# Mixture-of-experts layer on one core: tiles of 128 tokens, two tiles of any two experts per step, in place of pairs of tiles of one expert

## The chip, the cores and the metric

One core of one Trainium2 chip runs the program. The metric is the device time of one execution in microseconds, the median of the runs shown.

## The reference

The input is 8 sequences of 512 tokens with 256 features, fp32. A block of linear attention comes first and is not touched here; its result is added to the input and normalized. Then every token goes to 4 of 16 experts and to one shared expert:

```
weights, indices = gate(x)            # top 2 of 4 groups, then top 4 of 16 experts
h1 = x @ w1[e]; h3 = x @ w3[e]        # 256 -> 128, for the 4 chosen e
y  = sum_e c[e] * ((silu(h1) * h3) @ w2[e])        # 128 -> 256
z  = (silu(x @ ws1) * (x @ ws3)) @ ws2             # shared expert, 256 -> 256 -> 256
out = layernorm(x + y + z)
```

## The kernel before

All five queues are written out by hand, with semaphores between them. The work has three stages.

**Head (0 to 266 us).** Eight batches of 512 tokens pass through attention, first norm and routing. VectorE gives every (token, expert) a slot in a DRAM buffer `expert_in` with one region per expert (`assign_slots`), and GpSimd scatters the token rows there with indirect DMAs (`dispatch`, line 440). The batches form two waves of four; each wave has its own buffers. When a wave's counts are known, `plan_pairs` (lines 816 to 860) computes on VectorE which expert and which DRAM row each step takes: the region of an expert is cut into pairs of 256 rows, and the pairs of all experts are numbered through. With 64 tiles' worth of tokens and one partly filled pair per expert that makes at most 32 + 16 = 48 pairs per wave, and the program always runs all 48. Rows that no token fills are zeroed by SyncE (`fill_spare`, `fill_end`). The plan of wave 0 stands between the last batch and the shared expert (line 976); that of wave 1 is spread over the steps of wave 0 (`parts`, line 1089).

**Pair loop (266 to 593 us).** 96 steps, one pair each. For step g:
- SyncE (`load_xs`, line 325) reads the row from `pair_row` into a register, waits until the ring slot's earlier pair is transposed, and loads 256 rows (256 KB) into one of four `xs` tiles (in `kv`). `store_ys` (line 332) stores the result of an older pair.
- TensorE (`two_groups`, line 1375) transposes pair g + 2 (line 1340), reads the chunk number, that is the expert, of pair g into a register (`chunk_of`, line 1345), multiplies up (`up_pair`, line 1347) and then multiplies down pair g - 2 (`down_pair`, line 1360). Weights are split in a high and a low 16-bit part, and so are activations, so each product is three matmuls (`product`, lines 1149 to 1151). `we_hi[:, chunk, cols]` is addressed through the register. The loop body holds 8 steps; its first two read the chunk of pair g - 2 again.
- ScalarE splits and copies (lines 617, 624, 634, 642), VectorE forms the low parts and the product with silu (lines 1025, 1036, 1044).
- In wave 1, VectorE also adds wave 0's gathered results (`combine`) and normalizes them (`final_norm`, line 1065); GpSimd gathers them with indirect DMAs (line 452), each tile when `h_ready` reaches a number written in the program.

**Tail (593 to 705 us).** The last batches' shared expert, wave 1's gathers, combines and norms.

SyncE, ScalarE, VectorE and TensorE all write the loop in the same order of steps, most of it in hardware loops (`Fori`).

## Time and profile before

| | |
|---|---|
| median of 3 runs | 711.87 us (711.7 to 711.9) |
| the profiled execution's own time | 707.36 us |
| its span, first to last instruction | 705.5 us |
| granted TensorE clock, mean | 0.916 |
| busy: PE, DVE, ACT, POOL | 527.1, 427.4, 300.1, 290.1 us |
| bytes moved | 118.63 MB, mean 168 GB/s |

```text
span 705.5 us, 13461 instructions
## 1 busy us (share of the span) xinstructions
PE 527.1 (75%) x3532; PEld 357.0 (51%) x3555; DVE 427.4 (61%) x1200; ACT 300.1 (43%) x659; POOL 290.1 (41%) x334
## 2 busy tenths in 40 slices
PE   1899887889897688789786688798888779665400
PEld 1355443555544357567574566576667566421300
DVE  2447783776864866666554444377757556652784
ACT  2536653436524343555454555356546445110100
POOL 1000126456446402454444200644446251777574
PEclk9999997899999899999999999899999989977755
DMA  7022428295451303767767766687787753333332
GB/s 202 13 75 76 156 90 284 82 304 209 177 185 68 103 18 106 239 204 230 232 228 259 238 223 216 180 235 233 211 261 231 223 181 134 105 120 89 94 114 99
DMA packets 64091, 118.63 MB, mean 168 GB/s; under 512 B 9760, under 2 KB 23088, under 8 KB 64048
## 3 DMA queue, kind: packets, MB, share of 16 engines
q1 hardware_dynamic: 51216, 84.55, 37.1%
q0 software_dynamic: 12288, 33.57, 15.1%
q8 instruction: 19, 0.31, 0.2%
q14 instruction: 24, 0.20, 0.1%
q10 hardware_dynamic: 544, 0.00, 0.0%
HBM read 55.17 MB, written 62.91 MB: 167 GB/s over the span
## 4 chain that ended last, share of the span: by engine, by line
PE 36%; DVE 19%; issue 15%; SPq 9%; another core or an unknown queue 6%; ACT 6%; DMA 5%; POOL 4%; ACTq 0%; DVEq 0%; POOLq 0%
PE t L1340 4%; PE h_even L1149 4%; PE h_even L1151 4%; PE h_odd L1149 3%; PE h_even L1150 3%; PE h_odd L1151 3%; PE h_odd L1150 3%; DVE x_all L1055 2%; SPq L327 2%; PE y L1186 2%; DMA kv<-expert_in 2%; SPq L330 1%; PE y L1373 1%; SPq L334 1%
## 5 line engine op out<-in xcount | busy, mean ns | idle before, releaser
L440 POOL DMA_INDIRECT expert_in<-x_all,slots x128 | 132.9, 1038 | 117.8 <-PE h_odd L1151 45.0
L452 POOL DMA_INDIRECT wa_stage<-expert_out,result_of x64 | 62.9, 983 | 35.3 <-issue 18.1
L1340 PE MATMUL t<-ident,kv 128*128 128x128 f32 x384 | 60.3, 280 | 19.4 <-DMA kv<-expert_in 15.0
L452 POOL DMA_INDIRECT q_fm<-expert_out,result_of x32 | 32.4, 1014 | 85.6 <-DMA expert_out<-q_exp 63.9
L426 POOL TENSOR_SCALAR neg_mean<-mv 128x4 f32<-128x4 f32 x16 | 4.6, 290 | 149.5 <-DVE mv L699 149.3
L1044 DVE TENSOR_TENSOR wa_lo<-bias_heads,wa_hi 128x256 bf16<-128x256 f32 x96 | 40.5, 422 | 41.3 <-ACT wa_hi L642 30.1
L1149 PE MATMUL h_even<-xsT_hi,we_hi 128*128 128x256 f16 x192 | 54.3, 283 | 10.7 <-issue 8.8
L1340 PEld LDWEIGHTS t<-ident,kv 128*128 128x128 f32 x384 | 45.3, 145 | 26.8 <-DMA kv<-expert_in 12.1
L1025 DVE TENSOR_TENSOR xsT_lo<-t,xsT_hi 128x512 bf16<-128x512 f32 x72 | 49.5, 688 | 11.6 <-ACT xsT_hi L617 5.9
L1150 PE MATMUL h_even<-xsT_lo,we_hi 128*128 128x256 bf16 x192 | 54.2, 282 | 2.5 <-issue 2.5
L1151 PE MATMUL h_even<-xsT_hi,we_lo 128*128 128x256 f16 x192 | 54.2, 282 | 1.4 <-issue 1.4
L617 ACT ACTIVATE xsT_hi<-t 128x512 f16<-128x512 f32 x72 | 42.0, 585 | 16.6 <-PE t L1340 12.8
L642 ACT ACTIVATE wa_hi<-bias_heads 128x256 f16<-128x256 f32 x96 | 39.7, 414 | 20.7 <-DVE bias_heads L1036 14.4
L1036 DVE TENSOR_TENSOR bias_heads<-h_odd,kv_heads 128x256 f32<-128x256 f32 x48 | 20.2, 420 | 41.8 <-ACT kv_heads L634 40.9
L1036 DVE TENSOR_TENSOR bias_heads<-h_even,kv_heads 128x256 f32<-128x256 f32 x48 | 20.1, 419 | 34.4 <-ACT kv_heads L634 30.9
L634 ACT ACTIVATE kv_heads<-h_odd 128x256 f32<-128x256 f32 x48 | 18.3, 381 | 52.8 <-remote 25.0
L1186 PE MATMUL y<-wo_sb,gated 128*128 128x256 f32 x128 | 33.3, 419 | 9.3 <-DVE gated L686 9.3
L452 POOL DMA_INDIRECT gate<-expert_out,result_of x32 | 30.5, 954 | 19.4 <-PE h_even L1151 10.0
L529 ACT ACTIVATE kv<-h_even 128x256 f32<-128x256 f32 x32 | 12.3, 386 | 58.3 <-PE h_even L1151 52.4
L634 ACT ACTIVATE kv_heads<-h_even 128x256 f32<-128x256 f32 x48 | 18.2, 380 | 43.8 <-PE h_even L1151 17.4
L1367 PE MATMUL y<-we_hi,wa_hi 128*128 x96 | 26.8, 279 | 12.6 <-issue 10.7
L624 ACT ACTIVATE k_exp<-y 128x512 f32<-128x512 f32 x48 | 28.7, 598 | 15.9 <-PE y L1373 14.3
(222 smaller groups left out, 1530.0 us busy)
## 6 DMA issues: line engine op xcount, KB each, us to landing
kv<-expert_in SPq DMA_DIRECT2D x96, 256.0 KB
expert_out<-k_exp SPq DMA_DIRECT2D x48, 256.0 KB
expert_out<-q_exp SPq DMA_DIRECT2D x48, 256.0 KB
expert_in<-wa_stage SPq DMA_DIRECT2D x16, 512.0 KB
expert_in<-wa_stage SPq DMA_DIRECT2D x32, 256.0 KB
stage<-in_L_ffn_w SPq DMA_DIRECT2D x48, 128.0 KB
x_in<-in_L_attn_x SPq DMA_DIRECT2D x8, 512.0 KB
out<-gated SPq DMA_DIRECT2D x8, 512.0 KB
```

The costliest lines, as they stand in the source:

```text
L440: pool.indirect_dma_start(xs_dram[b // WB], bass.IndirectOffsetOnAxis(ap=slots[:, b, t, j:j + 1], axis=0), x_all[:, b, t, :], None).then_i ...
L452: pool.indirect_dma_start(y_got[i][:, j, :], None, ys_dram[w], bass.IndirectOffsetOnAxis(ap=result_of[:, b, t, j:j + 1], axis=0)).then_inc ...
L617: act.activation(xsT_hi[r][:, :, :], t_bank[r % 2][:, :].rearrange("p (c n) -> p c n", c=KC), ACT.Copy).then_inc(xst_hi_ready, 1)
L642: act.activation(aT_hi[r % 2][:, :], a_pair, ACT.Copy).then_inc(at_hi_ready, 1)
L1025: dve.tensor_tensor(xsT_lo[r][:, :, :], t_bank[r % 2][:, :].rearrange("p (c n) -> p c n", c=KC), xsT_hi[r][:, :, :], ALU.subtract).then_in ...
L1036: dve.tensor_tensor(a_pair, h_banks[r % 2][0][:, 2 * P:], s_pair, ALU.mult).then_inc(pair_a_ready, 1)
L1044: dve.tensor_tensor(aT_lo[r % 2][:, :], a_pair, aT_hi[r % 2][:, :], ALU.subtract).then_inc(at_lo_ready, 1)
L1149: pe.matmul(dst, sta_hi, mov_hi, start=start, stop=False)
L1150: pe.matmul(dst, sta_hi, mov_lo, start=False, stop=False)
L1151: return pe.matmul(dst, sta_lo, mov_hi, start=False, stop=stop)
L1186: last = pe.matmul(y_bank[h][:, (t % 2) * D:(t % 2 + 1) * D], gated[:, c, t * P:(t + 1) * P], wo_sb[:, c, :], start=c == 0, stop=c == KC - 1)
L1340: last = pe.transpose(t_bank[r % 2][:, c * 2 * P + i * P:c * 2 * P + (i + 1) * P], xs[r][:, i, c * P:(c + 1) * P], ident[:, :])
```

## The change

A step takes two tiles of 128 rows, each of any expert. Tiles are numbered through all experts, at most 64 + 16 = 80 per wave, and step p of a wave takes tiles p and p + 40: 40 steps a wave, 80 in all. Each tile has its own chunk and its own row. SyncE reads two rows and loads two halves of the `xs` tile (64 partitions with two rows each); the transposes write to every second column so that the halves stay apart; TensorE reads two chunks and multiplies up and down once per tile, with 128 columns in place of 256 in the up product. The plan works on 80 tiles per wave instead of 48 pairs and has one step more; the results' rows get one more operation. Half as many spare rows are zeroed. The 16 fills of wave 1's ends begin two groups earlier. GpSimd's fixed numbers change with the step count, and it waits for `out_ready` before three of its norm computations. The norms of wave 0's first three batches move from VectorE to ScalarE, and ScalarE's and VectorE's second wave is written out in place of hardware loops; the combines are spread evenly, from step 4 of the wave on.

```diff
-PLAN_STEPS = 8
+PLAN_STEPS = 9
...
-    NPAIR = WT * TOP_K // 2 + E
+    NTILE = WT * TOP_K + E
+    NPAIR = NTILE // 2
     PAIR = 2 * P
-    MOST = WB * S // PAIR
-    REGION = (MOST + 1) * PAIR
-    SPARE = NPAIR - WT * TOP_K // 2
-    SLOTS = E * REGION + SPARE * PAIR
+    MOST = WT
+    REGION = (MOST + 1) * P
+    SPARE = NTILE - WT * TOP_K
+    SLOTS = E * REGION + SPARE * P
     RING = 4
     GROUPS_OF_PAIRS = NPAIR // RING
     EARLY = WB - 1
-    PLAN_GROUPS = 7
+    PLAN_GROUPS = 8
+    NORM_PAIR = 17
     FILL_ROWS = 512
-    FILLS = SPARE * PAIR // FILL_ROWS
+    FILLS = SPARE * P // FILL_ROWS
...
-        pair_chunk = sb("pair_chunk", [1, WAVES * NPAIR, 1], I32)
-        pair_row = sb("pair_row", [1, WAVES * NPAIR, 1], I32)
+        tile_chunk = sb("tile_chunk", [1, 2, WAVES * NPAIR, 1], I32)
+        tile_row = sb("tile_row", [1, 2, WAVES * NPAIR, 1], I32)
...
             def load_xs(w, p, r, first=False):
-                row = sp.value_load(pair_row[0:1, NPAIR * w + p, :], min_val=0, max_val=SLOTS - PAIR)
+                rows = [sp.value_load(tile_row[0:1, h, NPAIR * w + p, :], min_val=0, max_val=SLOTS - P) for h in range(2)]
                 if not first:
                     sp.wait_ge(xs_transposed, NPAIR * w + p - RING + 1)
-                sp.dma_start(xs[r][:, :, :], rows_of(xs_dram[w], row)).then_inc(xs_loaded[r], 16)
+                for h in range(2):
+                    sp.dma_start(xs[r][h * P // 2:(h + 1) * P // 2, :, :],
+                                 rows_of(xs_dram[w], rows[h])).then_inc(xs_loaded[r], 16)
...
-                    pool.wait_ge(h_ready, NPAIR + (3 * k if k < WT - TT else 3 * WT - 13 + 2 * (k - WT + TT)))
+                    pool.wait_ge(h_ready, NPAIR + 9 * k // 4)
...
-                    pool.wait_ge(h_ready, 5 * i // 2)
+                    pool.wait_ge(h_ready, 2 * i)
...
-                        if b > 0 and t == (1 if w == 0 else TT - 1):
+                        if b > 0 and t == (2 if w == 0 else TT - 1):
+                            if 1 < b <= EARLY + 1:
+                                pool.wait_ge(out_ready, b - 1)
...
+            def final_norm(b, t):
+                if t == 0:
+                    act.wait_ge(rstd_ready, NB + b + 1)
+                    if b > 0:
+                        act.wait_ge(out_stored, 16 * b)
+                last = act.activation(o_sb[:, t, :], x_all[:, b, t, :], ACT.Identity, bias=shift[:, t:t + 1],
+                                      scale=rstd[:, t:t + 1])
+                if t == TT - 1:
+                    last.then_inc(out_ready, 1)
...
-            with act.Fori(1, all_groups // 2 - 1) as q2:
+            with act.Fori(1, GROUPS_OF_PAIRS // 2) as q2:
                 group(2 * q2)
                 group(2 * q2 + 1)
-            group(all_groups - 2)
-            group(all_groups - 1, last=True)
+            for p in range(NPAIR):
+                pair(NPAIR + p, p % RING, GROUPS_OF_PAIRS + p // RING, p < NPAIR - 2)
+                b, t = (p - NORM_PAIR) // 9, (p - NORM_PAIR) % 9
+                if 0 <= b < EARLY and t < TT:
+                    final_norm(b, t)
...
                 if part == 5:
                     dve.wait_ge(plan_step, at + 6)
-                    dve.scalar_tensor_tensor(closer[:, w, :], first_pair[:, :], float(PAIR), region_start, ALU.mult, ALU.subtract)
-                    dve.tensor_reduce(pair_expert_f[:, :], ended, AX_X, ALU.add)
-                    dve.tensor_tensor(skipped, ended, region_left[0:1, :].unsqueeze(1).to_broadcast([1, NPAIR, E]),
-                                      ALU.mult).then_inc(plan_step, 1)
+                    dve.scalar_tensor_tensor(closer[:, w, :], first_tile[:, :], float(P), region_start, ALU.mult, ALU.subtract)
+                    dve.tensor_reduce(tile_expert_f, ended, AX_X, ALU.add).then_inc(plan_step, 1)
                 if part == 6:
                     dve.wait_ge(plan_step, at + 7)
-                    dve.tensor_reduce(pair_row_f[:, :], skipped, AX_X, ALU.add).then_inc(plan_step, 1)
-                    dve.tensor_scalar(pair_chunk[:, NPAIR * w:NPAIR * (w + 1), 0], pair_expert_f[:, :], float(E - 1), float(SHARED),
+                    dve.tensor_tensor(ended, ended, region_left[0:1, :].unsqueeze(1).to_broadcast([1, NTILE, E]),
+                                      ALU.mult).then_inc(plan_step, 1)
+                    dve.tensor_scalar(tile_chunk[:, :, NPAIR * w:NPAIR * (w + 1), 0],
+                                      tile_expert_f.rearrange("p (h g) -> p h g", h=2), float(E - 1), float(SHARED),
                                       ALU.min, ALU.add).then_inc(experts_ready, 1)
                 if part == 7:
                     dve.wait_ge(plan_step, at + 8)
-                    dve.scalar_tensor_tensor(pair_row[:, NPAIR * w:NPAIR * (w + 1), 0], pair_no[0:1, :], float(PAIR),
-                                             pair_row_f[:, :], ALU.mult, ALU.add).then_inc(rows_ready, 1)
+                    dve.tensor_reduce(tile_row_f, ended, AX_X, ALU.add).then_inc(plan_step, 1)
+                if part == 8:
+                    dve.wait_ge(plan_step, at + 9)
+                    dve.scalar_tensor_tensor(tile_row[:, :, NPAIR * w:NPAIR * (w + 1), 0],
+                                             tile_no[0:1, :].rearrange("p (h g) -> p h g", h=2), float(P),
+                                             tile_row_f.rearrange("p (h g) -> p h g", h=2), ALU.mult, ALU.add).then_inc(rows_ready, 1)
...
+            group(PLAN_GROUPS + 1)
             dve.wait_ge(c_of_slot_ready, NB // 2)
             dve.wait_ge(shared_added, EARLY)
-            thirds = [((), (0,), (1, 2), (3, 4)), ((5,), (6,), (7, 8), (9,)), ((10,), (11, 12), (13,), (14, 15))]
-            halves = [[(8 * h + 2 * r, 8 * h + 2 * r + 1) for r in range(RING)] for h in range(2)]
-            group(q1)
-            for i in range(3):
-                group(q1 + 1 + i, 0, thirds[i])
-            with dve.Fori(1, EARLY) as b:
-                group(q1 + 1 + 3 * b, b, thirds[0])
-                group(q1 + 2 + 3 * b, b, thirds[1], norm=b - 1)
-                group(q1 + 3 + 3 * b, b, thirds[2])
-            group(q1 + 1 + 3 * EARLY, EARLY, halves[0], whole=False)
-            group(q1 + 2 + 3 * EARLY, EARLY, halves[1], norm=EARLY - 1, whole=False, last=True)
+            of_pair = [[i for i in range(WT * TOP_K) if 4 + 9 * i // 16 == p] for p in range(NPAIR)]
+            for p in range(NPAIR):
+                add = [(i // 16, i // TOP_K % TT, i % TOP_K) for i in of_pair[p]]
+                pair(NPAIR + p, p % RING, p < NPAIR - 2, add)
...
             def transpose_xs(g, r, use):
-                pe.wait_ge(xs_loaded[r], 16 * use)
+                pe.wait_ge(xs_loaded[r], 32 * use)
                 for c in range(KC):
+                    turned = t_bank[r % 2][:, c * PAIR:(c + 1) * PAIR].rearrange("p (k t) -> p k t", t=2)
                     for i in range(2):
-                        last = pe.transpose(t_bank[r % 2][:, c * 2 * P + i * P:c * 2 * P + (i + 1) * P],
-                                            xs[r][:, i, c * P:(c + 1) * P], ident[:, :])
+                        last = pe.transpose(turned[:, :, i], xs[r][:, i, c * P:(c + 1) * P], ident[:, :])
                 last.then_inc(xs_transposed, 1)
-            def chunk_of(g):
-                return pe.value_load(pair_chunk[0:1, g, :], min_val=SHARED, max_val=NCH - 1)
-            def up_pair(g, r, chunk):
+            def chunks_of(g):
+                return [pe.value_load(tile_chunk[0:1, h, g, :], min_val=SHARED, max_val=NCH - 1) for h in range(2)]
+            def up_pair(g, r, chunks):
                 if late(g, 2):
                     pe.wait_ge(pair_a_ready, g - 1)
-                for k in range(2):
-                    for c in range(KC):
-                        cols = slice((c * 2 + k) * INTER, (c * 2 + k + 1) * INTER)
-                        last = product(h_banks[r % 2][0][:, k * PAIR:(k + 1) * PAIR],
-                                       we_hi[:, chunk, cols], we_lo[:, chunk, cols],
-                                       xsT_hi[r][:, c, :], xsT_lo[r][:, c, :], c == 0, c == KC - 1)
+                for h, chunk in enumerate(chunks):
+                    tok = slice(h * P, (h + 1) * P)
+                    for k in range(2):
+                        for c in range(KC):
+                            cols = slice((c * 2 + k) * INTER, (c * 2 + k + 1) * INTER)
+                            last = product(h_banks[r % 2][0][:, k * PAIR + h * P:k * PAIR + (h + 1) * P],
+                                           we_hi[:, chunk, cols], we_lo[:, chunk, cols],
+                                           xsT_hi[r][:, c, tok], xsT_lo[r][:, c, tok], c == 0, c == KC - 1)
                 last.then_inc(h_ready, 1)
-            def down_pair(g, r, chunk):
+            def down_pair(g, r, chunks):
                 pe.wait_ge(at_lo_ready, g + 1)
                 if late(g, 2):
                     pe.wait_ge(ys_copied, g - 1)
-                w2_hi, w2_lo = we_hi[:, chunk, W13:], we_lo[:, chunk, W13:]
-                dst, tok = y_bank[r % 2][:, 0:D], slice(0, P)
-                pe.matmul(dst, aT_hi[r % 2][:, tok], w2_hi, start=True, stop=False)
-                pe.matmul(dst, aT_lo[r % 2][:, tok], w2_hi, start=False, stop=False)
-                pe.matmul(dst, aT_hi[r % 2][:, tok], w2_lo, start=False, stop=True)
-                dst, tok = y_bank[r % 2][:, D:], slice(P, PAIR)
-                pe.matmul(dst, aT_hi[r % 2][:, tok], w2_lo, start=True, stop=False)
-                pe.matmul(dst, aT_hi[r % 2][:, tok], w2_hi, start=False, stop=False)
-                pe.matmul(dst, aT_lo[r % 2][:, tok], w2_hi, start=False, stop=True).then_inc(ys_ready, 1)
+                for h, chunk in enumerate(chunks):
+                    last = product(y_bank[r % 2][:, h * D:(h + 1) * D],
+                                   aT_hi[r % 2][:, h * P:(h + 1) * P], aT_lo[r % 2][:, h * P:(h + 1) * P],
+                                   we_hi[:, chunk, W13:], we_lo[:, chunk, W13:], True, True)
+                last.then_inc(ys_ready, 1)
             def two_groups(q, last=False):
                     pe.wait_ge(xst_lo_ready, g + 1)
                     if not (last and i >= 2 * RING - 2):
                         transpose_xs(g + 2, (r + 2) % RING, q + 1 + (i + 2) // RING)
-                    chunks.append(chunk_of(g))
+                    chunks.append(chunks_of(g))
                     up_pair(g, r, chunks[i])
                     if i >= 2:
                         down_pair(g - 2, (r - 2) % RING, chunks[i - 2])
                     elif late(q, 1):
-                        down_pair(g - 2, (r - 2) % RING, chunk_of(g - 2))
+                        down_pair(g - 2, (r - 2) % RING, chunks_of(g - 2))
                 return chunks[-2:]
```

## Rows read from the trace of the kernel before

**Rows 1.** The page, busy time of each engine.
```profile
PE 527.1 (75%) x3532; PEld 357.0 (51%) x3555; DVE 427.4 (61%) x1200; ACT 300.1 (43%) x659; POOL 290.1 (41%) x334
```

**Rows 2.** Busy time by stage, two windows.
```profile
core 0: us, PE busy (x) PEld busy (x) DVE busy (x) ACT busy (x) POOL busy (x), PEclk, DMA share, GB/s
266.00:593.00 327.00, 266.15 (x2138) 210.08 (x2137) 193.31 (x496) 167.93 (x384) 127.34 (x136) 0.96 0.68 216
384.00:404.00 20.00, 14.04 (x114) 10.58 (x112) 7.79 (x16) 9.24 (x21) 7.36 (x8) 1.00 0.77 248
```

**Rows 3.** Line 1340, whole span, then 560.5 to 570.4, then 384 to 404.
```profile
L1340 PE MATMUL t<-ident,kv x384: 269/273/421, 266.3 to 581.7; 128*128 128x128 f32 x192
...
L1340 PEld LDWEIGHTS t<-ident,kv x19: 139/141/143, 560.6 to 570.4; 128*128 128x128 f32 x19
...
L1340 PE MATMUL t<-ident,kv x24: 272/273/331, 383.8 to 404.0; 128*128 128x128 f32 x24
```

**Rows 4.** PE's sequencer and weight loads by line, 564.27 to 567.04: durations ns min/median/max, starts.
```profile
L1345 PEldq TENSOR_LOAD <-pair_chunk x2: 297/300/302, 564.4 to 566.0; - x2
...
L1149 PEldq FUSED_REGOPS  x4: 46/46/46, 565.0 to 565.8; - x4
L1149 PEld LDWEIGHTS h_odd<-xsT_hi,we_hi x4: 98/98/98, 565.8 to 566.8; 128*128 x4
...
L1151 PEldq ALU_OP  x4: 32/32/32, 565.2 to 565.9; - x4
...
L1364 PEldq EVENT_SEMAPHORE  x1: 51/51/51, 566.7 to 566.7; - x1
...
L1367 PEldq FUSED_REGOPS  x1: 60/60/60, 566.8 to 566.8; - x1
...
L1337 PEldq EVENT_SEMAPHORE  x2: 51/51/51, 564.3 to 567.0; - x2
```

**Rows 5.** Timeline of the weight loads at 401 us: start us, us.
```profile
401.56 0.10 PEld L1151 LDWEIGHTS h_odd<-wa_hi,we_lo 128*128 x1
401.71 0.10 PEld L1149 LDWEIGHTS h_odd<-wa_hi,we_hi 128*128 x1
401.78 0.10 PEld L1150 LDWEIGHTS h_odd<-wa_lo,we_hi 128*128 x1
```

**Rows 6.** Line 1345, chunk loads of the whole span.
```profile
L1345 PEldq TENSOR_LOAD <-pair_chunk x118: 10/311/1293, 269.6 to 585.1; - x118
```

**Rows 7.** Timeline of PE at 251 us, matmuls of 16 columns.
```profile
251.06 0.24 PE L1225 MATMUL t<-sel_all,ones 128*128 128x16 f16 x4
```

**Rows 8.** Timeline of PE at 446 us.
```profile
446.50 0.27 PE L1149 MATMUL h_odd<-xsT_hi,we_hi 128*128 128x256 f16 x1 [0.38 <-issue]
447.24 0.27 PE L1150 MATMUL h_odd<-xsT_lo,we_hi 128*128 128x256 bf16 x1 [0.47 <-issue]
```

**Rows 9.** SyncE's queue by line: a step at 505 us, an end fill at 401 us.
```profile
L334 SPq DMA_DIRECT2D expert_out<-q_exp x1: 333/333/333, 505.2 to 505.2; - x1
...
L327 SPq TENSOR_LOAD <-pair_row x1: 268/268/268, 505.5 to 505.5; - x1
...
L330 SPq DMA_DIRECT2D kv<-expert_in x1: 350/350/350, 506.2 to 506.2; - x1
...
L296 SPq TENSOR_LOAD <-fill_row x1: 268/268/268, 401.3 to 401.3; - x1
...
L297 SPq DMA_DIRECT2D expert_in<-wa_stage x1: 333/333/333, 402.0 to 402.0; - x1
```

**Rows 10.** The chain that ended last, at 232 to 237 us.
```profile
232.23 0.92 DVE stage L844
...
236.20 0.68 DVE x_in L986
```

**Rows 11.** Lines of the plan, both waves.
```profile
L844 DVE TENSOR_TENSOR stage<-plan_sb,pairs_end x2: 940/963/986, 232.2 to 312.0; 1x768 f32<-1x768 f32 x2
...
L835 DVE TENSOR_TENSOR stage<-n_pairs,plan_sb x2: 418/421/424, 231.1 to 305.6; 128x256 f32<-128x256 f32 x2
```

More of the change, by code:

```diff
@@ L1026, in xst_lo, with pair @@
                                   xsT_hi[r][:, :, :], ALU.subtract).then_inc(xst_lo_ready, 1)
-            def pair(g, r, ahead=True, add=None, norm=None, whole=True, part=None):
+            def pair(g, r, ahead=True, add=(), part=None):
                 if ahead:
@@ L1073, in final_norm, with group @@
                     last.then_inc(out_ready, 1)
[L1075 removed]
+            def group(q, parts=()):
                 for r in range(RING):
[L1078 to L1082 removed]
+                    pair(RING * q + r, r, part=parts[r] if r < len(parts) else None)
             xst_lo(0, 0)
```

103 lines of the change are left out of this document (48 added, 55 removed).

## Prediction

> **What bounds the kernel now.** I read the busy table first: TensorE is busy for 75% of the span, VectorE 61%, so no engine is full [rows 1]. The table by stage then shows where the change acts. The pair loop runs from 266 to 593 us, 327 us of the 705.5, and holds 96 steps [rows 2]: line 1340 has 384 transposes, four a step, from 266.3 to 581.7 us [rows 3]. The stage divided by the steps is 3.40 us per step. The stretch 560.6 to 570.4 us shows what a step costs when nothing waits: its 19 transposes are four whole steps and three transposes more, so (9.8 - 0.2)/4 = 2.4 us a step [rows 3]. That is the array's own need: 12 up matmuls, 6 down matmuls and 4 transposes packed end to end, 2.40/22 = 0.109 us from start to start. So 1.0 us of a step is lost.
>
> The rows of PE's sequencer say more. In one step at 564.3 to 567.0 us it does, in order: the semaphore, the chunk load (TENSOR_LOAD at 564.4, register operations, check, first address of line 1149 at 565.0), four products (a register operation at line 1149 and an ALU_OP at line 1151 each), another chunk load at 566.0, and the semaphore at 566.7, the address of the down product (566.8) and the next step's semaphore at 567.0 [rows 4]. From it I take three prices: **a chunk load costs 0.65 us** of sequencer time (566.0 to 566.7, likewise 564.4 to 565.0; only 0.30 is the load itself), **a product of three matmuls costs 0.24 us** (565.0 to 566.0 for four), and the down part 0.35 us. This step without the reload is 2.7 - 0.65 = 2.1 us; 118 loads for 96 steps [rows 6] add 0.23 x 0.65 = 0.15; loop branches lie on top. The sequencer needs 2.25 to 2.4 us per step, as much as the array: the two are balanced now. That the 0.24 is the sequencer's own pace and not a full queue's shows where the array is caught up: the second weight load of line 1149 starts at 401.71, 0.15 us behind the one before it (line 1151, 401.56), and the next follows after 0.07 [rows 5]; the array had been ready and the instruction came late.
>
> **Parts of the change.** *Fewer steps:* 96 to 80. At today's 3.40 us this is 16 x 3.40 = 54 us off, if a step stays as long.
>
> *Up product of two tiles:* 24 matmuls of 128 columns in place of 12 of 256. The trace has no 16-bit matmul of 128 columns. Below it, matmuls of 16 columns start 0.025 us apart (x4 in 0.24 with a last one of 0.17) [rows 7]; above it 256 columns take 0.109 (as above). The array's part of the up is therefore between 24 x 0.025 = 0.6 and 24 x 0.109 = 2.6 us; columns times rate give 1.31, as now. The addresses are a different matter: each of the eight products (tile, k, c) has its own chunk, so the sequencer computes eight pairs of addresses instead of four: +4 x 0.24 = **+0.96 us per step**. Nothing hides this: the sequencer is already even with the array, and with 128 columns the array finishes a product in 0.16 us, sooner than the next is issued.
>
> The Trainium skill, page "TensorE: Matmul & The Clock Gate", section "Wait — 56ns, not 53.3ns?", says that a warm matmul of 128 columns starts every 55.6 ns and that matmuls go to the engine without sequencer microcode. By that alone the split is free, the step keeps its length, and the outcome is rival A below. The trace agrees on the floor of 25 ns; the rows of register operations between the matmuls are what the rule leaves out.
>
> *Second chunk load:* each step reads two chunks, and the reload at the head of the two groups reads two as well: +1.23 x 0.65 = **+0.80 us per step**. Bounds: 0.65 each if it runs free; the load alone has a median of 0.31 but reaches 1.29 us in the whole loop [rows 6]. At the low end it costs nothing, if the second load ran under the first.
>
> The Trainium skill, page "DMA: Bandwidth & Descriptors", section "Latency and other measured facts", gives a floor of about 0.6 us for a tensor_load. This trace shows 0.30 us; by the page's figure a step would be about 0.3 us longer for each load.
>
> *Down product:* two products with own chunks, where six matmuls shared two addresses: +0.24 us.
>
> *Sum of a step:* 2.40 + 0.96 + 0.80 + 0.24 = 4.40 us of sequencer. On top come interruptions. Of the 1.0 us that a step loses now, part is waits (for xs tiles, for the first gathered rows), which a slower PE would meet less; part is the sequencer itself: at 446.5 and 447.24 us single matmuls start 0.7 us apart with "issue" as reason [rows 8], and loads stretch to over 1 us. Bounds 0 and 1.0; I take 0.55, just over the middle, because a step has more instructions than now. So **4.95 us x 80 = 396 us**, against 327 now.
>
> *Clock:* the array would work 2.4 of 4.95 us. In 384 to 404 us there are six steps (24 transposes) of 3.4 us, with PE busy 14.0 of 20 us, at a granted clock of 1.00; over the stage it is 0.96 [rows 2, 3]. Falls are likely here and there, at no great price: at 1.2 GHz the array's 4.8 us still fit.
>
> *SyncE:* at 505 to 507 us a step is a store (issue 0.33), a row load (0.27, with its checks until the issue at 506.2) and an issue (0.35) [rows 9], 1.5 us from 505.2 to 506.6 with a little around it. A second row load and issue add 0.65 + 0.4: 2.5 us. The 16 end fills, now two groups earlier, each add about 1.2 us (a load at 401.3, an issue at 402.0 of 0.33) [rows 9]: 3.7 us. Even with the interruptions this stays under 4.95, so loads arrive ahead and the two waits around the second wave go under PE. The halved DMAs move the same bytes per step, and 16 steps of 512 KB and half the fills go: no bound at 0.68 DMA share now [rows 2].
>
> *Plan:* for wave 0 it is on the path: the chain passes line 844 at 232.23 us and three operations of the same size (849, 850, 854) before x_in of line 986 at 236.20 [rows 10]. Line 844 takes 0.96 us on 768 elements [rows 11]; with 1280, 1.6: +2.5 us for four. Two operations double to 256 elements, 0.28 to 0.42 as line 835 [rows 11], and one step of the plan more: in all **+3 us**. For wave 1 the plan lies in pairs whose VectorE is idle 41% (193 of 327 us busy [rows 2]): nothing. The additional operation in the results likewise.
>
> *Norms on ScalarE:* 12 operations in a loop where ScalarE is busy 168 of 327 us [rows 2]: nothing, even at 1 us each; the cover is gone only if a step fell to some 2 us. The new POOL wait for out_ready stands behind work finished 9 pairs before; behind it are only gathers with 10 us each. *Combine:* it begins at pair 4 of the wave rather than 5, but in slower steps: nothing if the first gather has landed by then, at worst one wait of a step, 5 us, inside the range. Strided transposes write the same 128 columns: 0 to 0.44 us a step, into an array that idles. Tail (593 to 705 us): same work, 0.
>
> **The sum.** The profiled execution took 707.4 us (span 705.5): 707.4 + 3 - 327 + 396 = 779.4. Its time lies 4.5 us under the median of 711.87, so against that median: **784 us**.
>
> **Rivals.**
> A, *the step keeps its length* (faster). Mechanism: PE's queue holds enough matmuls that address arithmetic and chunk loads of the second tile run under the array. Price: 80 x 3.40 = 272; 707.4 + 3 - 327 + 272 + 4.5 = 660 us. It decides for faster from a step under (327 - 3)/80 = 4.05 us. For it: the sequencer does run ahead, line 1149's addresses at 565.0 to 565.8 against its weight loads at 565.8 to 566.8 [rows 4], and 1.0 us of the step is slack. Against: 4.40 us of sequencer operations in series in rows 4; a queue cannot hide the slower of its two ends. 10%.
> B, *only the second load is hidden*: 3.60 + 0.55 = 4.15 us, 332 us in the loop, 720 us. 10%.
> C, *interruptions grow with the instructions*: the whole 1.0 us stays, 5.40 us, 432 us, 820 us. VectorE's and ScalarE's second wave also turns from loops into straight code. 13%.
> That the steps do not fall to 80 is no rival: the count is fixed in the program. Between A and B, within 0.2% of before: 2%.
>
> **Numbers.** My forecast, 4.95 us with its interruptions from 0.2 to 0.9 us, has 65%. The lower end of the range, 735, is 4.40 us with almost no interruption (352 us: 740, less a few for the waits); the upper, 815, nearly reaches C. About 0.2% (1.4 us) is what a measurement of this kernel can tell from no change. Slower: 65 + 13 + most of B, 0.87; same 0.02; faster 0.11, A and a low B.
>
> **What would show it.** The spacing of the first transposes near 4.9 us with few DMA waits before them; two TENSOR_LOADs in series per step, 0.65 us apart; address pairs of line 1149 and 1151 still 0.24 us apart, and matmuls bunched in threes with gaps of 0.07 us; idle of PE put down to "issue"; lines 844 to 854 near 1.6 us. Steps under 4.05 us, or loads that overlap, would make the prediction wrong.

## The result, and the profile after

The changed kernel takes **800.05 us** (median of 4 runs, 794.7 to 807.6) against 711.79 for the kernel before: ratio 1.122, interval 1.114 to 1.131. The forecast was 784 us with a range of 735 to 815. One of the four runs, 807.6 us, counts as a slow one, and the ratio is that of the others. The profiled execution took 796.3 us, 794.6 of them span.

The page's row of busy times, after:

```profile
PE 558.8 (70%) x4140; PEld 373.7 (47%) x4163; DVE 410.1 (52%) x1142; ACT 280.7 (35%) x607; POOL 289.2 (36%) x334
```

PE and its weight loads are busy for 32 and 17 us more than before [rows 1] in a span 89 us longer; VectorE and ScalarE are busy for 17 and 19 us less, GpSimd for as long as before. No engine is near full. Next, busy time by stage:

```profile
core 0: us, PE busy (x) PEld busy (x) DVE busy (x) ACT busy (x) POOL busy (x), PEclk, DMA share, GB/s
268.00:672.00 404.00, 288.84 (x2674) 220.01 (x2671) 170.37 (x430) 144.52 (x323) 126.12 (x136) 0.88 0.46 147
672.00:794.60 122.60, 55.86 (x297) 30.53 (x300) 68.34 (x174) 15.63 (x29) 71.49 (x84) 0.72 0.32 104
```

The pair loop takes 404 us against 327 [rows 2], and PE is busy for 289 us of it. The granted clock there is 0.88, against 0.96 before. The transposes place it more exactly, and the chunk loads are the instruction suspected:

```profile
L1353 PEld LDWEIGHTS t<-ident,kv x320: 137/141/231, 268.1 to 665.9; 128*128 128x128 f32 x160
...
L1357 PEldq FUSED_REGOPS  x356: 3/151/725, 272.1 to 674.4; - x178
L1357 PEldq TENSOR_LOAD <-tile_chunk x196: 3/302/783, 271.5 to 674.0; - x196
```

The four transposes of a step are at line 1353 now (1340 before). 320 of them from 268.1 to 665.9 us are 79 steps and three transposes: (397.8 - 0.4)/79 = **5.03 us per step**. The weight loads of before are these:

```profile
L1340 PEld LDWEIGHTS t<-ident,kv x384: 138/141/230, 266.2 to 581.5; 128*128 128x128 f32 x192
```

The same sum on them, (581.5 - 266.2 - 0.4)/95, gives 3.31 us. The 89.1 us of span divide into +1.9 ahead of the first transpose (266.2 to 268.1), +82.5 from the first to the last, and +4.7 behind the last (124.0 to 128.7).

What one step consists of, PE's sequencer from 450.1 to 454.3 us, by line (durations ns min/median/max, first and last start):

```profile
L1357 PEldq TENSOR_LOAD <-tile_chunk x2: 300/302/303, 450.2 to 451.0; - x2
L1357 PEldq SEQ_ASSERT  x2: 18/18/18, 450.8 to 451.5; - x2
...
L1161 PEldq FUSED_REGOPS  x10: 46/46/46, 451.6 to 453.9; - x10
...
L1163 PEldq ALU_OP  x8: 32/32/32, 451.8 to 453.5; - x8
...
L1378 PEldq EVENT_SEMAPHORE  x1: 51/51/51, 453.6 to 453.6; - x1
...
L1349 PEldq EVENT_SEMAPHORE  x1: 51/51/51, 454.3 to 454.3; - x1
```

The two loads start at 450.2 and 451.0, the second's check is at 451.5, then come eight register operations of line 1161 for the up part and two for the down part (451.6 to 453.9), eight ALU_OPs of line 1163, the semaphore of line 1378 at 453.6 and the next step's at 454.3. Nothing is waited for, and it takes 4.1 us; with the step's own semaphore and transposes ahead of this window, from 450.0 us on, it is 4.3. A step that also reads the chunks of the step two back once more has two loads on top. How the array receives it, timeline of the weight loads (start us, us):

```profile
451.96 0.10 PEld L1161 LDWEIGHTS h_odd<-wa_hi,we_hi 128*128 x1
451.97 0.10 PEld L1162 LDWEIGHTS h_odd<-wa_lo,we_hi 128*128 x1
452.08 0.10 PEld L1163 LDWEIGHTS h_odd<-wa_hi,we_lo 128*128 x1
452.22 0.10 PEld L1161 LDWEIGHTS h_odd<-wa_hi,we_hi 128*128 x1
452.24 0.10 PEld L1162 LDWEIGHTS h_odd<-wa_lo,we_hi 128*128 x1
452.31 0.10 PEld L1163 LDWEIGHTS h_odd<-wa_hi,we_lo 128*128 x1
452.46 0.10 PEld L1161 LDWEIGHTS h_odd<-wa_hi,we_hi 128*128 x1
```

Each product is three matmuls, and from one line 1161 to the next it is 0.26 and 0.24 us: the array takes what it gets and stands still for the rest. What PE waited for in the loop:

```profile
PE h_even L1161 <- issue: 36.7, 32, 4.4
PE y L1161 <- issue: 27.8, 21, 2.4
PE h_odd L1161 <- issue: 17.2, 20, 1.7
PE h_odd L1161 <- DVE bias_heads L1062: 10.7, 9, 1.8
...
PE h_even L1161 <- DVE bias_heads L1062: 7.3, 7, 2.1
PE t L1353 <- DMA kv<-expert_in: 2.4, 3, 1.4
```

The idle time before L1161, the first matmul of each product, is put down to "issue" (36.7 + 27.8 + 17.2 = 82 us; before, at lines 1149 and 1367, it was 27). The wait for the xs tiles, kv<-expert_in, has gone down to 2.4 us: the loads arrive ahead. Before it was

```profile
PE t L1340 <- DMA kv<-expert_in: 15.0, 11, 3.8
```

### The profile page after: what moved, and what is told of

It is laid out like the page before. It is cut to its first block, busy times and chain, and to the rows that moved or that the text cites. A ratio compares the mean times of both kernels' runs of the same rounds, so it can differ in the third digit from the quotient of the medians.

```text
span 794.6 us, 15510 instructions
## 1 busy us (share of the span) xinstructions
PE 558.8 (70%) x4140; PEld 373.7 (47%) x4163; DVE 410.1 (52%) x1142; ACT 280.7 (35%) x607; POOL 289.2 (36%) x334
## 4 chain that ended last, share of the span: by engine, by line
PE 31%; issue 21%; DVE 17%; SPq 10%; another core or an unknown queue 9%; ACT 6%; POOL 3%; DMA 3%; ACTq 0%; DVEq 0%; POOLq 0%
PE h_even L1161 5%; PE h_odd L1161 4%; SPq L328 3%; PE h_even L1163 3%; PE h_even L1162 3%; SPq L332 3%; PE t L1353 3%; PE y L1198 2%; PE h_odd L1163 2%; PE y L1161 2%; DVE x_all L1079 2%; PE h_odd L1162 2%; PE y L1163 1%; PE y L1162 1%
## 5 line engine op out<-in xcount | busy, mean ns | idle before, releaser
L1161 PE MATMUL h_even<-xsT_hi,we_hi 128*128 128x128 f16 x320 | 79.1, 248 | 44.1 <-issue 36.7
L1161 PE MATMUL y<-we_hi,wa_hi 128*128 (+1 forms) x192 | 58.4, 304 | 39.9 <-issue 32.5
L1163 PE MATMUL h_even<-xsT_hi,we_lo 128*128 128x128 f16 x320 | 77.6, 243 | 0.2 <-issue 0.2
L1162 PE MATMUL h_even<-xsT_lo,we_hi 128*128 128x128 bf16 x320 | 77.6, 243 | 0.0
L1161 PEld LDWEIGHTS h_even<-xsT_hi,we_hi 128*128 x320 | 33.9, 106 | 66.4 <-issue 54.3
L1162 PE MATMUL y<-we_lo,wa_hi 128*128 (+1 forms) x192 | 57.7, 301 | 4.6 <-issue 4.6
L1163 PE MATMUL y<-we_hi,wa_lo 128*128 (+1 forms) x192 | 57.6, 300 | 3.5 <-issue 3.5
L1161 PE MATMUL h_odd<-xsT_hi,we_hi 128*128 128x128 f16 x160 | 41.2, 263 | 13.6 <-issue 8.7
L1161 PE MATMUL h_odd<-wa_hi,we_hi 128*128 128x128 f16 x160 | 37.8, 236 | 15.8 <-issue 8.5
L1161 PEld LDWEIGHTS y<-we_hi,wa_hi 128*128 128x128 f16 x192 | 20.3, 106 | 56.6 <-issue 52.4
```

The lines of the kernel that those rows point to most:

```text
L1161: pe.matmul(dst, sta_hi, mov_hi, start=start, stop=False)
L1162: pe.matmul(dst, sta_hi, mov_lo, start=False, stop=False)
L1163: return pe.matmul(dst, sta_lo, mov_hi, start=False, stop=stop)
```

## The experiments

Theory T: TensorE's sequencer sets the pace, with its addresses and chunk loads in series. Rivals: the array (matmuls of 128 columns), SyncE with its doubled row loads and transfers, and interruptions that grow with the code. The kernel before took 702.9, 645.6 and 648.2 us on the chips of the three groups of runs, so every ratio below is to the kernel before of the same chip. The expectations of the first two groups were written in microseconds of the first chip (711.8 us); they are compared as ratios. "Per step" is worked out from line 1353 or 1340 as above; the "fast tenth" is the spacing that a tenth of the steps' first transposes keep or undercut, the first two spacings, where the loop starts, left out (before 2.40, after 4.05 us).

**First group: one suspected cost put into the kernel before** (before: 702.9 us).

The split alone, all else as before:

```diff
-for k in range(2):
-    for c in range(KC):
-        last = product(h[:, k * PAIR:(k + 1) * PAIR], w(chunk, c, k), xsT[r][:, c, :], ...)
+for h in range(2):
+    tok = slice(h * P, (h + 1) * P)
+    for k in range(2):
+        for c in range(KC):
+            last = product(h[:, k * PAIR + h * P:...+ P], w(chunk, c, k), xsT[r][:, c, tok], ...)
```

> The kernel before, with the up product alone cut in two halves of 128 columns, both with the pair's one chunk: 24 matmuls and eight address pairs where there were 12 and four. Same 96 steps, one chunk load, the result unchanged. My theory (TensorE's sequencer sets the pace, 0.24 us for a product of three matmuls with its addresses): the sequencer's own need rises from 2.40 to 3.35 us a step; with 0.6 to 0.9 us of waits and interruptions 4.0 to 4.2 us a step, 385 to 405 us in the loop, 770 to 790 us in all. Rival (the array sets the pace, and 24 x 128 columns are 12 x 256): 712 us. Second rival (waits for SyncE and the chain hide most of it, since a step takes 3.40 us already): 720 to 740 us.

> The kernel before, with the up product cut in two halves of 128 columns as in the run above, but in an order in which both halves use the same weight address: 24 matmuls with only four address pairs. The second half's products go to another PSUM bank that is not read, so half of each pair's hidden values are stale. My theory (the addresses cost, not the matmuls of 128 columns): the array's 2.40 us a step do not change, and the sequencer has 24 more plain instructions; 712 to 735 us. Rival (the additional matmuls and weight loads cost by themselves, up to 0.109 us each): up to 12 x 0.109 x 96 = 125 us more, 837 us; halfway between would be 775 us.

The second kernel puts both halves behind one address pair by hand; it also has one more wait ahead of the loop's first step (`prefixed`). Measured: **725.3 us**, ratio 1.034 (1.025 to 1.043), and **724.9 us**, 1.035 (1.029 to 1.042). The first misses its 770 to 790 us (1.08 to 1.11) and lies where its second rival had it; the second is at the upper end of its 712 to 735 (1.00 to 1.03). The build computes an address once for the same chunk and columns: the first kernel has 384 register operations at line 1149, as many as before. So it also had only four address pairs, and its expectation tested nothing of the addresses; the two are one measurement. Weight loads of the second one, timeline at 300 us:

```profile
300.38 0.10 PEld L1360 LDWEIGHTS h_odd<-xsT_hi,we_hi 128*128 x1
300.44 0.10 PEld L1361 LDWEIGHTS h_odd<-xsT_lo,we_hi 128*128 x1
300.49 0.10 PEld L1360 LDWEIGHTS h_odd<-xsT_hi,we_hi 128*128 x1
300.55 0.10 PEld L1361 LDWEIGHTS h_odd<-xsT_lo,we_hi 128*128 x1
300.60 0.15 PEld L1363 LDWEIGHTS h_odd<-xsT_hi,we_lo 128*128 x2
```

With addresses for two products at once, the weight loads of matmuls of 128 columns start every 0.056 us, half of the 0.109 of a matmul of 256: the columns cost what they did. The fast tenth stays at 2.43 us. So the array does not explain most of the 88 us; the +22 us in the mean are discussed below.

Every chunk load twice (one more value_load ahead of the old one):

> The kernel before, with every chunk load done twice, the first value unused: 236 loads in place of 118. Nothing else changes, the result neither. My theory (loads run in series in the sequencer, 0.65 to 0.75 us each, nothing hides them): the sequencer needs 2.40 + 0.85 = 3.25 us a step, a step takes 3.9 to 4.1 us, 375 to 395 us in the loop, 760 to 780 us in all. Rival (a second load runs under the first or under the array's work): 712 to 720 us.

Measured: **735.7 us**, 1.049 (1.041 to 1.057). The fast tenth goes from 2.40 to 2.91 us. From one semaphore of line 1337 to the next, a step without reload took the sequencer 2.3 us before where it was not held up, and takes 2.98 now (median of the 61 without reload and loop branch). So a load is in series, at 0.7 us, and a little of it used slack: the array alone needs 2.4. The rival, a hidden load, fails. The expected 760 to 780 us (1.07 to 1.10) are missed too: the sequencer needs 0.77 x 2.98 + 0.23 x 4.90 (its steps with reload) = 3.42 us, and the mean step is 3.67, so only 0.25 us came on top and not the 0.65 to 0.85 expected. The waits of the kernel before go under a slower sequencer.

The changed kernel with one chunk load per step:

```diff
-return [pe.value_load(tile_chunk[0:1, h, g, :], ...) for h in range(2)]
+chunk = pe.value_load(tile_chunk[0:1, 0, g, :], ...)
+return [chunk, chunk]
```

> The changed kernel with one chunk load per step instead of two; both tiles of a step use the first tile's expert, so the second tile's hidden values are those of a wrong expert. Addresses, matmuls and DMAs as in the changed kernel. My theory: 100 loads of 0.75 us fewer, 75 us off: about 725 us, somewhat more (up to 745) if SyncE's 3.5 to 4.9 us per step becomes the next bound. Rival (the second load is hidden): 800 us.

Measured: **746.5 us**, 1.064 (1.055 to 1.074), where the whole change has 1.122 on another chip. With equal chunks the addresses also fall from eight pairs to four (and in the down part from two to one; line 1161 has 400 register operations in place of 800), so this takes away two costs of T together. The ratio is still above what was expected (at most 745 us, 1.047). What is left over before is now another wait, of PE on kv<-expert_in, 49.0 us: SyncE.

**Second group: TensorE against SyncE** (before: 645.6 us).

Four kernels with 80 steps. "TensorE as before" has one chunk load, up products of 256 columns and the old down part (the second tile thus uses the first tile's expert). "SyncE light" has one row load and one transfer of 256 KB, from x and not from the gathered rows. Both leave the routing out of what they touch.

```diff
-rows = [sp.value_load(tile_row[0:1, h, NPAIR * w + p, :], ...) for h in range(2)]
-for h in range(2):
-    sp.dma_start(xs[r][h * P // 2:(h + 1) * P // 2, :, :], rows_of(xs_dram[w], rows[h])).then_inc(...)
+row = sp.value_load(tile_chunk[0:1, 0, NPAIR * w + p, :], ...)
+sp.dma_start(xs[r][:, :, :], x...[bass.ds(row, PAIR), :]...).then_inc(xs_loaded[r], 16)
```

> The changed kernel with SyncE's work per step as before the change: one register load and one DMA of 256 KB into all 128 partitions. It reads from the input x at a row number that is the chunk's, so the tokens are not the dispatched ones. TensorE as in the changed kernel. My theory (TensorE's sequencer is the bound, SyncE runs ahead except where it fills): 780 to 800 us, and the waits of TensorE for xs tiles go. Rival (SyncE, whose step takes 3.5 us and with a fill 4.9 us, sets the pace in much of the loop): 16 steps x 0.7 us in the fill stretch and more elsewhere, 750 us or less.

> The changed kernel with TensorE's step as before the change: one chunk load, the up product with 256 columns, the down product with two addresses, the second tile with the first tile's expert. SyncE keeps two row loads and two DMAs per step, 80 steps. It undoes TensorE's part alone. My theory: TensorE's need falls to 2.4 us, and SyncE becomes the bound: 64 steps of 3.5 and 16 of 4.9 us with fills, about 300 us in the loop, 700 us in all. Rival (SyncE hides its work, the step returns to 3.40 us): 272 us in the loop, 665 us.

> Both together: TensorE's and SyncE's step as before the change, 80 steps (tokens from the input x as in the run with one DMA, one expert per step). It is what fewer steps would be worth if a step kept its length: 272 us in the loop, 660 us in all by the rival of my prediction. My theory gives the same number, 655 to 675 us, since only the step's content lengthened it. If it stays over 690 us, something else in the change (the norms on ScalarE, the loops written out, the plan) costs too.

> The changed kernel with fixed chunks (2 and 3) in the up product: the eight address pairs per step vanish, both chunk loads stay, 24 matmuls of 128 columns as before; the hidden values are those of fixed experts. My theory: the sequencer saves up to 8 x 0.16 = 1.3 us a step (the 0.24 less what three matmuls need on the array, 0.16, or less), so 0.6 to 1.3 us x 80 = 50 to 100 us off: 700 to 750 us; if SyncE then is the bound, 730 to 750. Rival (the pace is that of the matmuls of 128 columns and their weight loads, not of the addresses): 800 us.

| | TensorE as before | fixed chunks in the up part | TensorE as changed |
|---|---|---|---|
| SyncE light | **609.3** (0.943) | | **746.1** (1.155) |
| SyncE as changed | **678.7** (1.050) | **686.2** (1.062) | **745.2** (1.152, third group) |

The intervals are within 0.012 of each ratio. Read along the first row, TensorE's part costs 746.1 - 609.3 = 137 us if SyncE is light; read down the right column, SyncE's part costs nothing while TensorE is slow; down the left one it costs 69 us. The two are limits side by side, not a sum. Against the expectations: one transfer with TensorE as changed was expected at 1.10 to 1.12 by the theory and at 1.05 or less by the rival (750 us of 711.8); 1.155 is above both, and nothing was gained, as the theory says. Both light, 0.92 to 0.95 was expected and 0.943 came out. TensorE light alone was expected at 700 us, 0.98, and is at 1.050: its loop has about the length expected (304 us for 300), but the kernel before is 66 us faster on this chip than on the first, which the expectation did not allow for. Fixed chunks save 59 us, as expected (50 to 100), but end at 1.062, just above the 1.054 at most. The waits say the same. What SyncE and PE waited for in the kernel of 678.7 us:

```profile
SPq L337 <- ACT k_exp L629: 3.6, 4, 1.9
SPq L337 <- ACT q_exp L629: 1.3, 4, 0.5
...
PE t L1353 <- DMA kv<-expert_in: 48.9, 48, 2.7
```

and SyncE in the changed kernel, third group:

```profile
SPq L337 <- ACT q_exp L629: 47.4, 26, 3.8
SPq L337 <- ACT k_exp L629: 28.6, 24, 5.5
```

SyncE waits for results to store 76 us in the changed kernel and 5 us once TensorE is quick: then it hardly rests, and PE waits 48.9 us for it. SyncE's own work, a step with a fill in the changed kernel, 452.7 to 457.6 us:

```profile
L328 SPq TENSOR_LOAD <-tile_row x2: 362/413/464, 452.8 to 453.7; - x2
...
L332 SPq DMA_DIRECT2D kv<-expert_in x2: 468/485/502, 454.5 to 455.2; - x2
...
L299 SPq TENSOR_LOAD <-fill_row x1: 271/271/271, 455.8 to 455.8; - x1
...
L300 SPq DMA_DIRECT2D expert_in<-wa_stage x1: 527/527/527, 456.5 to 456.5; - x1
...
L337 SPq DMA_DIRECT2D expert_out<-k_exp x1: 447/447/447, 457.2 to 457.2; - x1
```

That is 4.9 us, of which the fill takes 1.4 (455.7 to 457.0): 3.5 us without it. In the kernel of 678.7 us the 16 steps with a fill are 5.1 us apart and the others 3.6. An issue for 64 partitions takes 0.47 to 0.53 us here (transfers and fill), while the one for 128 before took 0.35 [rows 9]; over all steps the medians of the transfers are 0.474 and 0.349.

Fixed chunks in the up part (both tiles with constant experts, loads kept) take only the addresses away, and are at 686 us, in SyncE's limit too. So at least 59 of the 97 us hang on the addresses of the up part; how much more can't be seen, since SyncE stops the gain.

**Third group: the addresses by themselves, and a candidate** (before: 648.2 us).

> The changed kernel itself once more, beside the others of this job on the same chip, because the kernel before took between 646 and 712 us on different chips. Both theories: 1.12 to 1.14 times the kernel before of the same chip, a step of about 5 us with a fastest one near 4.0.

Measured: **745.2 us**, 1.152 (1.147 to 1.157), above the expected 1.12 to 1.14.

The kernel before, split, with the second half two columns further on, which makes eight address pairs of four:

```diff
-cols = slice((c * 2 + k) * INTER, (c * 2 + k + 1) * INTER)
+at = (c * 2 + k) * INTER + 2 * h
+cols = slice(at, at + INTER)
```

> The kernel before, its up part in two halves of 128 columns as in the earlier split, but the second half takes its weights two columns further on, so that eight address pairs are worked out and not four; those products are off by two columns of the weights. One chunk load and SyncE's work stay as before. Theory: the sequencer needs 2.4 + 0.96 = 3.35 us per step, a mean step of about 4.1 us: 50 to 75 us over the 22 us that the split alone cost, so 70 to 100 us over before. Rival (addresses are free): 22 us over before, as the split with four pairs.

Measured: **711.3 us**, 1.098 (1.093 to 1.102). Its transposes:

```profile
L1340 PEld LDWEIGHTS t<-ident,kv x384: 137/141/230, 256.9 to 591.2; 128*128 128x128 f32 x192
```

(591.2 - 256.9 - 0.4)/95 = 3.51 us per step, the fast tenth 3.26. No SyncE work was added, the chunk load is one, the matmuls are those of the split, and the register operations at line 1149 are 768 in place of 384: the split with four address pairs more costs 63 us. Between its semaphores of line 1337 the sequencer needs 3.3 us (median of the 61 steps without reload and loop branch) and 4.1 with a reload, so 0.77 x 3.3 + 0.23 x 4.1 = 3.5: it alone makes the 3.51. It is 7 us under the expected band, since on this chip hardly anything came on top. How much of the 63 the split alone would cost here was not tried; at the 3.5% of the first group it would be 22.

The changed kernel with shared addresses (second tile's up product uses the first chunk):

```diff
-for h, chunk in enumerate(chunks):
+for h in range(2):
+    chunk = chunks[0]
```

> The changed kernel, but the up products of both tiles use the weights of the first tile's expert, so the second tile's up product is of the wrong expert; both chunk loads stay, and the down products too. TensorE then works out four address pairs in the up part and not eight. Theory (TensorE's sequencer sets the pace): 4 x 0.24 = 0.96 us less per step, the fastest steps at 3.1 in place of 4.0 us; SyncE, at 3.5 us a step and 4.9 with a fill, becomes the bound of some steps, so 40 to 75 us below the changed kernel. Rival (addresses lie under the array, and SyncE or the gathers set the pace): the same time as the changed kernel within 10 us.

Measured: **699.8 us**, 1.080 (1.076 to 1.084), 45 us under the changed kernel, at the low end. Fast tenth 3.24 us, mean 4.10. SyncE's wait for results has fallen from 76 to 22.8 us, and the 16 steps with a fill are 4.98 us apart where the others are 3.95 apart (5.02 and 4.66 in the changed kernel): the steps with a fill gain nothing, since SyncE is now their limit, the others gain 0.71 us, and the mean gains 0.55 and not 0.96.

The candidate: the kernel before with TensorE's pair loop written out, so that load addresses are constants and the chunks of the two pairs behind stay in registers.

```diff
-elif late(q, 1):
-    down_pair(g - 2, (r - 2) % RING, chunk_of(g - 2))
+elif late(q, 1):
+    down_pair(g - 2, (r - 2) % RING, old[i])
...
-with pe.Fori(1, GROUPS_OF_PAIRS // 2) as q2:
-    two_groups(2 * q2)
+for q2 in range(1, GROUPS_OF_PAIRS // 2):
+    old = two_groups(2 * q2, old=old)
```

> A candidate to beat both: the kernel before with TensorE's loop over the pairs written out, each step with its load addresses as constants and the chunks of the two pairs behind kept in registers, so that 22 of the 118 chunk loads and the branches go. Theory: 22 x 0.75 = 14 us less of the sequencer, some of it under other waits: 5 to 15 us below before. Rival (the short halts of the sequencer come with straight code that has to be fetched): no gain, or up to 20 us slower, with more halts of about 0.7 us than in the loop.

Measured: **639.5 us**, 0.987 (0.983 to 0.992): 8.7 us under before, and 106 under the changed kernel of the same chip. Its chunk loads and transposes:

```profile
L1345 PEldq TENSOR_LOAD <-pair_chunk x96: 297/540/1192, 263.3 to 526.4; - x96
...
L1340 PEld LDWEIGHTS t<-ident,kv x384: 136/141/232, 259.9 to 522.3; 128*128 128x128 f32 x192
```

96 loads in place of 118; (522.3 - 259.9 - 0.4)/95 = 2.76 us per step. It is 1.3% under the kernel before, little but clear of the noise. Loads, branches and load addresses went together, so what each gave is not shown. That the halts come with straight code is not borne out here, but this chip shows no halt with any kernel (last section), so on a chip with halts it stays untested.

## Why the prediction was right, and where its terms were off

**The sign and the mechanism.** The forecast said that the sequencer and the array were balanced and that addresses and loads in series would make 4.95 us a step; 5.03 were measured. The signs named beforehand are there: spacing near 4.9 us, few DMA waits, two TENSOR_LOADs in series (0.75 us apart and not 0.65), bunches of three matmuls 0.24 us apart, idle put down to "issue". Only the wide operations of the plan are at 1.39 to 1.48 us and not near 1.6. That it is the sequencer and not the array is shown by the split with shared addresses (fast tenth unchanged) against the one with shifted addresses (0.83 us more).

**Addresses, +0.96 us.** The fast tenth rose by 3.26 - 2.43 = 0.83 us for four pairs, and the sequencer's own step, 3.3 us with eight pairs, is 3.3 - 0.95 = 2.35 with four: 0.1 us of the addresses went under the array, which needs 2.40. The price of 0.24 us per product holds, as the weight loads 0.24 to 0.26 apart show.

**Second load, +0.80 us.** Loads start 0.75 apart, not 0.65: the estimate left out the register operation that forms the load's address. 1.23 x 0.75 = 0.92.

**Down product, +0.24 us.** In the step shown the sequencer spends 0.68 us on it (from the semaphore of line 1378 at 453.58 to the next step's at 454.26), where the step of rows 4 spends 0.36 (566.68 to 567.03): +0.32.

**Sum.** 4.40 was forecast. On the third group's chip, where hardly anything else comes in, the sequencer takes 4.3 us from one wait of line 1349 to the next (median of the 51 steps without reload and loop branch) and 6.0 in the 18 steps with a reload (5.3 to 6.4): 0.775 x 4.3 + 0.225 x 6.0 = 4.68. The 0.28 too little are about 0.12 for the loads, 0.08 for the down product, and the rest in the step before, put at 2.40 with its reloads where 2.35 + 0.23 x 0.75 = 2.52 was needed.

**Interruptions, +0.55 us.** On the profiled chip 5.03 - 4.68 = 0.35; on the third group's (622.3 - 254.4 - 0.4)/79 = 4.65, so nothing. So rival C, that the whole 1.0 us stays, fails, and rival B fails with both loads in series. The sum was 0.28 too low and this term 0.20 too high, and they nearly offset each other. The mechanism was right; that the step came within 0.08 us is in part luck, since the 0.55 was a choice between bounds of 0 and 1.0. Part of the 0.35 is a wait that the forecast did not have, of the up products for VectorE (bias_heads, 10.7 + 7.3 us in the fence, 0.2 us a step); it is 0.8 us in all on the other chip.

**Clock, "no great price".** The granted clock of the loop is 0.88 on the profiled chip and 0.93 on the third group's. On the first, 28 of 77 steps lie for more than a tenth in a stretch at the lower level, 1.2 GHz; they are 5.5 us apart in the mean, the other 49 4.9. On the other chip 17 steps do, at 5.5 us, and the other 60 are at 4.5. If the falls alone made those steps longer, they would cost 28 x 0.65 = 18 us on the profiled chip, which would be part of the 0.35 us a step. Whether they do, or a step in which PE idles lets the clock fall, no run separates. The falls are not the difference between the chips, which is there at full clock as well.

**SyncE, "stays under".** It does, but by much less than the sum gave: 2.5 and 3.7 us were forecast, 3.5 and 4.9 measured. The terms that failed are the second issue (0.4 for what takes 0.66 with its register operations), the loads (0.65 for 0.85 and 0.74), and the first issue and the store, which were taken as unchanged and went from 0.50 to 0.69 and from 0.38 to 0.63. With the fill it reaches the 4.95 us forecast; in those steps a quicker TensorE gains nothing, as the 5.1 us of the kernel of 678.7 us show. Rival A failed twice over: even with TensorE's old step, 80 steps took 5% longer than 96.

**Plan, +3 us.** Chain that ended last, after:

```profile
231.70 1.40 DVE stage L861
...
233.29 1.39 DVE stage L866
234.71 1.48 DVE stage L869
...
236.30 1.41 DVE stage L876
...
237.89 0.68 DVE x_in L1012
```

The four wide operations take 1.39 to 1.48 us in place of 0.85 to 0.94 (the first is in rows 10): from the first to x_in 6.19 us against 3.97, +2.2; the first transpose is 1.9 us later.

**Tail, 0.** It is +4.7 us on the profiled chip. On the third group's chip the changed kernel has 742.7 - 622.3 = 120.4 us behind the last transpose and the written-out kernel before 638.5 - 522.3 = 116.2: +4.2 (the split with shifted addresses has 117.5). Two steps are still in work when the last tile is transposed, and each is longer by 1.7 us; this accounts for most of it, by argument only.

**The 17 us too few.** 779.4 us were forecast for the profiled execution and 796.3 measured. The tail has 4.7 of the difference, the plan takes 1.1 off, and 80 x (5.03 - 4.95) = 6.4 are in the step. The last 7 are a slip of the stage's bounds: 327/96 = 3.40 was called the step, though the spacing is 3.31. The window of 327 us holds 11.5 us behind the last transpose, which the forecast took away with the steps and which stayed; of these its eightieth step gives back 4.6, since there are 79 spacings. The median lies 3.7 us above the profiled execution.

**The rule on matmul issue.** The Trainium skill, "TensorE: Matmul & The Clock Gate", section "Wait — 56ns, not 53.3ns?", says that warm matmuls of 128 columns start 55.6 ns apart and go straight to the engine. The 0.056 us of the split with shared addresses agrees. It holds for matmuls whose addresses are there; with an address of their own for every three, products start 0.24 us apart and not 3 x 0.056 = 0.17.

**The rule on loads.** The Trainium skill, "DMA: Bandwidth & Descriptors", section "Latency and other measured facts", gives about 0.6 us as floor of a tensor_load. The 196 loads of the changed kernel have a median of 0.302 us, so the floor does not hold here. The forecast had gone by the trace.

**What stays open.** The split alone costs 22 us in the mean though not in the fast tenth. In the first of the two kernels PE's idle before the third matmul of a product, put down to "issue", is up (h_odd at line 1151: 7.7 us in 11 waits, against 0.5 before); whether it would cost this much on a chip without halts was not tried. The clock is part of the picture: in the two splits 23 and 18 of 93 spacings lie for more than a tenth in a stretch at 1.2 GHz, against 9 in the kernel before on the first chip (the kernel before has no trace on the splits' chip), and the loop's granted clock is 0.92 and 0.93 against 0.96. The spacings at full clock have the same mean in all three, 3.2 us, so by this comparison the additional time sits in the steps in which the clock fell. Which of the two brings the other is not shown. A version that shares addresses where both tiles have the same expert was not tried either.

## What to carry to other kernels

Before two products of one step get weights of their own, count the instructions of the issuing sequencer: here 0.24 us per product with an address from a register and 0.75 us per value loaded, against 0.17 us of array for three matmuls of 128 columns. Fewer and fuller steps, with the rest of the change, were worth 5.7% (609.3 against 645.6 us) where neither queue had to name a second expert, and both queues that had to name the second expert, PE's and SyncE's, took more than that back. Where a loop is bound so, take loads and address arithmetic out of it (22 loads, the loop branches and the load addresses fewer: 1.3%) rather than waste out of the array.

## What the runs showed of the hardware that was not expected

The same kernel before took 711.8, 702.9, 648.2 and 645.6 us on four chips. The rows of one tiny register instruction of SyncE's queue tell two kinds of chip apart (ns min/median/max): the kernel before on the first chip, the changed one with one chunk on the chip of the first group, the written-out one on that of the third:

```profile
L330 SPq MOVE kv<-expert_in x96: 3/29/724, 237.0 to 569.7; - x96
...
L332 SPq MOVE kv<-expert_in x160: 2/29/721, 243.8 to 618.3; - x160
...
L330 SPq MOVE kv<-expert_in x96: 29/29/38, 229.8 to 516.7; - x96
```

A MOVE of 29 ns takes up to 0.72 us on the two slower chips, and never over 38 ns on the fast one. Over all traces, SyncE's longest MOVE is 0.71 to 0.78 us in each of the six on the chips of 711.8 and 702.9 us, and 42 or 43 ns in each of the eight on the chips of 648.2 and 645.6. PE's queue shows it too, though less often (on the first group's chip only in the kernel that loads twice): line 1357's register operations reach 725 ns in the changed kernel of the first chip, and on the third group's chip

```profile
L1357 PEldq FUSED_REGOPS  x356: 37/151/165, 258.4 to 630.8; - x178
```

the longest is 165 ns. So the halts go with the chip and not with the kernel. They fit a step of the changed kernel of 5.03 us on one chip and 4.65 on the other with a fast tenth of 4.05 on both, but no run shows that they make the whole difference. What causes them is open. The penalty of the change is 88 us on the first chip and 97 on the one without halts; why it is not smaller there is open.
